# Linear attention over chunks: masked scores times v and q times the state, as one product over 128 rows

## The reference

```python
def _L0_attn_ref(x, W_attn, b_attn, W_proj, b_proj):      # 16 heads of 32, T = 1024 steps
    q, k, v = jnp.split(x @ W_attn + b_attn, 3, axis=-1)
    q = elu(to_heads(q)) + 1; k = elu(to_heads(k)) + 1; v = to_heads(v)
    def step(carry, inp):
        kv, ksum = carry
        qt, kt, vt = inp
        kv = kv + kt[..., :, None] * vt[..., None, :]
        ksum = ksum + kt
        num = jnp.einsum('bhi,bhij->bhj', qt, kv)
        den = jnp.einsum('bhi,bhi->bh', qt, ksum)[..., None] + EPS
        return ((kv, ksum), num / den)
    ...
    return y @ W_proj + b_proj
x = L0_attn_x                                             # (8, 1024, 512) f32
x = x + _L0_attn_ref(_layernorm(x), W_attn, b_attn, W_proj, b_proj)
x = x + _L0_ffn_ref(_layernorm(x), ffn_weight, ffn_bias)  # fp8-rounded x times fp8-rounded weight
```

## Time and profile before

| what | value |
|---|---|
| median of 3 runs | 1015.83 us (1012.76 to 1016.66) |
| the profiled execution | 1014.31 us, span 1012.6 us |
| PE busy | 982.0 us, 97% of the span |
| DVE, POOL, ACT busy | 701.7, 535.3, 463.6 us |
| mean granted clock of PE | 0.991 |

### The profile page before, as it was taken

The page is one execution under the profiler, slowest core; times in us unless marked ns, Lnnn a source line. Parts: engine busy times, 40 slices in busy tenths (PEclk is TensorE's granted clock), DMA queues, the critical chain, the costliest instruction groups (busy, mean ns, idle before and its releaser), DMA issues.

```text
span 1012.6 us, 43583 instructions
## 1 busy us (share of the span) xinstructions
PE 982.0 (97%) x19504; PEld 549.5 (54%) x19504; DVE 701.7 (69%) x1448; ACT 463.6 (46%) x714; POOL 535.3 (53%) x523
## 2 busy tenths in 40 slices
PE   5999999999999999999999999999999999999895
PEld 2454555555555555555555555555555555555552
DVE  6888677677767677676767767767776767754573
ACT  5753452544545364453535445254454535445222
POOL 3545675564565565465456456456456556533323
PEclk9999999999999999999999999999999999999997
DMA  8714334333334334334342244343332543322211
GB/s 271 113 35 80 94 76 81 86 77 84 80 75 91 75 75 94 72 83 88 71 96 74 71 93 79 78 88 75 83 83 75 90 77 75 81 44 54 55 35 48
DMA packets 185355, 82.51 MB, mean 81 GB/s; under 512 B 165840, under 2 KB 165840, under 8 KB 185168
## 3 DMA queue, kind: packets, MB, share of 16 engines
q1 hardware_dynamic: 185168, 79.73, 34.9%
HBM read 22.81 MB, written 16.78 MB: 39 GB/s over the span
## 4 chain that ended last, share of the span: by engine, by line
PE 91%; DVE 3%; POOL 2%; ACT 1%; issue 1%; DMA 0%; ACTq 0%; POOLq 0%
PE R L231 74%; PE S L231 15%; PE R L235 3%; POOL st L875 1%; DVE st L606 1%; DVE xs L696 0%; POOL xn L877 0%; POOL x L877 0%; DVE raw L800 0%; DMA xs<-in_L_attn_x 0%; POOL xs L918 0%; POOL sm L902 0%; DVE qk L629 0%; DVE wpl L778 0%; ACT qk L448 0%
## 5 line engine op out<-in xcount | busy, mean ns | idle before, releaser
L231 PE MATMUL R<-xt,wh 128*128 128x512 f16 x1024 | 306.2, 381 | 2.4 <-ACT wh L439 2.4
L629 DVE SCALAR_TENSOR_TENSOR qk<-qk,rel 128x512 f32<-128x512 f32 x128 | 141.3, 1105 | 151.1 <-ACT rel L451 151.1
L909 POOL TENSOR_TENSOR yhl<-y,yhl 128x512 f16<-128x512 f32 x60 | 69.9, 1165 | 311.2 <-ACT yhl L439 311.2
L231 PE MATMUL R<-xt,wl 128*128 128x512 f16 x512 | 194.4, 381 | 0.0
L875 POOL TENSOR_TENSOR st<-st,half 128x1 f32<-128x1 f32 x128 | 94.8, 741 | 138.3 <-DVE st L611 125.4
L231 PE MATMUL R<-wh,xt 128*128 128x512 f16 x512 | 160.3, 379 | 0.0
L231 PEld LDWEIGHTS R<-xt,wh 128*128 128x128 f16 x1024 | 96.7, 98 | 108.4 <-DVE xt L744 2.6
L231 PE MATMUL R<-wph,yt 128*128 128x512 f16 x512 | 134.6, 386 | 2.8 <-DVE yt L689 2.8
L439 ACT ACTIVATE yhl<-y 128x512 f16<-128x512 f32 x60 | 37.8, 630 | 209.5 <-DVE y L683 209.5
L448 ACT ACTIVATE qk<-R,bqk,wm 128x512 f32<-128x512 f32 x128 | 98.9, 772 | 54.0 <-PE R L231 54.0
L897 POOL TENSOR_TENSOR xs<-xs,bp 128x512 f32<-128x512 f32 x64 | 110.4, 1731 | 0.1
(11 more groups left out here) (91 smaller groups left out, 1498.0 us busy)
## 6 DMA issues: line engine op xcount, KB each, us to landing
xs<-in_L_attn_x SPq DMA_DIRECT2D x64, 256.0 KB, 3.8
out<-xs SPq DMA_DIRECT2D x64, 256.0 KB, 2.4
raw<-in_L_attn_W_attn SPq DMA_DIRECT2D x3, 1024.0 KB, 9.6
xs<-in_L_attn_W_proj SPq DMA_DIRECT2D x4, 256.0 KB
raw<-in_L_ffn_weight SPq DMA_DIRECT2D x1, 1024.0 KB, 16.2
x2t<-x2b SPq DMA_TRANSPOSE x62, 2.3
xt<-xnhl SPq DMA_TRANSPOSE x60, 3.1
yt<-yhl SPq DMA_TRANSPOSE x60, 3.2
```

What stands on the lines that cost most here:

```text
L231: return e.matmul(out, a, b, start=start, stop=stop, skip_group_check=True)
L629: e.scalar_tensor_tensor(qk[j % 2][:, i, :], qk[j % 2][:, i, :], 1.0, rel[:, (u - 1) % 2, :], ALU.min, ALU.add).then_inc(s_phi, 1)
L909: e.tensor_tensor(yhl[:, n % 2, 1, :], y[:, :], yhl[:, n % 2, 0, :], ALU.subtract).then_inc(s_yl, 1)
```

## The change

`from_state` goes. For each tile `sm` holds, for both halves a, 128 rows: in the 64 rows of the half itself the masked scores, and in the other 64 rows q (two heads' 32 rows one above the other). Facing them, v1 holds v in the 64 rows of the half and in the other 64 rows the state's 32 rows of the head, with zeros in the 32 rows of its neighbour. One product of 128 rows then gives both parts, and Y is written whole, 32 queries at a time: 64 products of 128 rows, 32 x 33.

- PE: `values(n)` is 64 such products (128 instructions); `from_state` (64 instructions, 32 in the first tile of a sequence) and the old `values` (64) are gone.
- DVE: `scores(n)` is two products of 64 partitions x 1024 columns, ahead of `ln1(n+8)`; `v_out` is two instructions of 64 partitions in place of one; y is one product of 128x512; `ln1_parts` moves to POOL. Between sequences the state is set to zero by a memset.
- ACT: the sm copy goes. `queries(n+1)` (four copies, 64 partitions x 512) stands behind the last phi of tile n and waits for `values(n)` on PE (`s_av`); `spread(n+1)` (eight copies, 32 partitions x 132) stands behind the copy of y and waits for mid and state of `update(n+1)` on DVE.
- POOL: the mask goes, `ln1_parts(n+8)` comes, behind `add_bp(n+8)`.
- `v1` is a ring of five tiles (NV) with a copy for each half; at the start POOL zeroes it whole and sets the ones. `sm` is now in the space of the raw v weights.

```diff
-            def from_state(n):
+            def values(n):
                 src, v, j, c = parts(n)
...
+                pe.wait_ge(s_smd, n + 1)
+                pe.wait_ge(s_q, n + 1)
+                pe.wait_ge(s_v, n + 1)
+                pe.wait_ge(s_spread, n + 1)
                 for g in range(4):
...
+                    for h in range(4):
+                        for i in range(4):
+                            a, b = divmod(i, 2)
+                            at = g * HALF + 32 * b
+                            mm = matmul(Y[32 * i:32 * i + 32, h, g * W:(g + 1) * W], sm[:, h, a, at:at + 32],
+                                        v[:, a, 4 * g + h, :], True, True)
                 mm.then_inc(s_av, 1)
...
@@ PE, in each tile
                 if n < NT:
                     scores(n)
-                    from_state(n)
                     ahead(chunks(n)[0])
...
@@ ACT
-            def scores(n):
-                if not alone(n):
-                    act.wait_ge(s_score, 4 * n + 4)
-                    if n:
-                        act.wait_ge(s_av, n)
-                    copy(sm[:, 2:4, :, :], scored(2)).then_inc(s_scopy, 1)
+            def queries(n):
+                src, v, j, c = parts(n)
+                for g in range(4):
+                    act.wait_ge(s_phi, phi_count(j, g))
+                act.wait_ge(s_wl, 6)
+                if n:
+                    act.wait_ge(s_av, n)
+                for a in range(2):
+                    for p in range(2):
+                        q = src[half_rows(p), 0:4, tokens(n, a)[0]].unsqueeze(1).broadcast_to([HALF, 2, 4, HALF])
+                        dst = sm[half_rows(1 - a), 2 * p:2 * p + 2, a, :].rearrange("p h (g t) -> p h g t", g=4)
+                        made = copy(dst, q)
+                made.then_inc(s_q, 1)
+            def spread(n):
+                v = v1[:, n % NV, :, :, :].rearrange("p a (g h) w -> p a g h w", g=4)
+                act.wait_ge(s_one, 2)
+                if n >= NV:
+                    act.wait_ge(s_av, n - NV + 1)
+                for a in range(2):
+                    act.wait_ge(*((s_mid, n + 1) if a else (s_state, n + 1)))
+                    held = mid if a else state[:, n % 2, :]
+                    for h in range(4):
+                        at, rows = HALF * (1 - a) + 32 * (h % 2), slice(32 * h, 32 * h + 32)
+                        made = copy(v[at:at + 32, a, :, h, :], held[rows, :].rearrange("p (g w) -> p g w", g=4))
+                made.then_inc(s_spread, 1)
...
@@ ACT, in each tile
-                    scores(n)
...
                     if n:
                         ahead(chunks(n)[1])
+                    if n + 1 < NT:
+                        queries(n + 1)
                     values(n)
                     if n == 0:
                         ahead(chunks(n)[1])
+                    if n + 1 < NT:
+                        spread(n + 1)
...
@@ DVE
             def scores(n):
...
+                for a in range(2):
+                    dst = sm[half_rows(a), :, a, :].rearrange("p h (g t) -> p h g t", g=4)
+                    made = e.tensor_tensor(dst, scored(a), causal_over(a), ALU.mult)
+                made.then_inc(s_smd, 1)
...
-                e.tensor_tensor(dst[:, 0:4:2, :, :], out[:, 0:4:2, :, 0:32],
-                                inv[:, 0:4:2, :, :].broadcast_to([P, 2, 4, 32]), ALU.mult)
...
+                e.tensor_tensor(dst, out[:, :, :, 0:32], inv.broadcast_to([P, 4, 4, 32]), ALU.mult).then_inc(s_y, 1)
...
@@ DVE, in each tile
                 if n < NT:
+                    scores(n)
                     if n + 8 < NT:
                         ln1(n + 8)
-                    scores(n)
...
-                    if n + 8 < NT:
-                        ln1_parts(n + 8)
...
@@ POOL
                     if n + 8 < NT:
                         ln1(n + 8)
-                    scores(n)
                     if n + 8 < NT:
                         add_bp(n + 8)
+                        ln1_parts(n + 8)
...
+            e.memset(v1[:, :, :, :, :], 0.0).then_inc(s_blank, 1)
```

More of the change, by code:

```diff
@@ L323, in scores @@
                             rows = slice(32 * h, 32 * h + 32)
-                            matmul(S[out, h, g * HALF:(g + 1) * HALF], src[rows, 4 + g, cols], src[rows, g, cols], True, True)
-            def from_state(n):
[L328 to L342, removed]
+                            mm = matmul(S[out, h, g * HALF:(g + 1) * HALF], src[rows, 4 + g, cols], src[rows, g, cols],
+                                        True, True)
@@ L344, in values @@
+                mm.then_inc(s_score, 1)
             def values(n):
                 src, v, j, c = parts(n)
-                first = n % PER == 0
-                pe.wait_ge(s_smd, masked_dve(n))
-                if not alone(n):
-                    pe.wait_ge(s_sel, n)
+                pe.wait_ge(s_smd, n + 1)
+                pe.wait_ge(s_q, n + 1)
                 pe.wait_ge(s_v, n + 1)
[L351 to L357, removed]
+                pe.wait_ge(s_spread, n + 1)
@@ L569, in _ @@
             phi(0, 7)
+            queries(0)
+            k_tokens(0)
             proj_size()
-            k_tokens(0)
             ffn_half()
@@ new lines, in v_out @@
+                dve.wait_ge(s_one, 2)
+                if n >= NV:
+                    dve.wait_ge(s_av, n - NV + 1)
+                for a in range(2):
+                    rows = half_rows(a)
+                    made = e.scalar_tensor_tensor(v1[rows, n % NV, a, :, 0:32], heads(bank["qkv", j, 8 + t][rows, :]),
+                                                  UN_V[rows], heads(bv[rows, :]), ALU.mult, ALU.add)
+                made.then_inc(s_v, 1)
+            def scores(n):
+                dve.wait_ge(s_score, n + 1)
+                dve.wait_ge(s_causal, 3)
+                if n:
+                    dve.wait_ge(s_av, n)
+                for a in range(2):
+                    dst = sm[half_rows(a), :, a, :].rearrange("p h (g t) -> p h g t", g=4)
+                    made = e.tensor_tensor(dst, scored(a), causal_over(a), ALU.mult)
+                made.then_inc(s_smd, 1)
@@ L658, in update @@
                 if n % PER < PER - 1:
                     dve.wait_ge(s_mid, n + 1)
-                    e.tensor_tensor(new, bank["delta", n, 1][:, 0:4 * W], mid[:, :], ALU.add).then_inc(s_state, 1)
+                    e.tensor_tensor(state[:, (n + 1) % 2, :], bank["delta", n, 1][:, 0:4 * W], mid[:, :],
+                                    ALU.add).then_inc(s_state, 1)
+                elif n + 1 < NT:
+                    e.memset(state[:, (n + 1) % 2, :], 0.0).then_inc(s_state, 1)
             def values(n):
@@ L897, in add_bp @@
                 e.tensor_tensor(x, x, bp[:, :], ALU.add).then_inc(s_xb, 1)
-            def scores(n):
-                if not alone(n):
-                    pool.wait_ge(s_scopy, n)
-                    e.tensor_tensor(sm[:, 2:4, :, :], sm[:, 2:4, :, :], causal_over(2), ALU.mult).then_inc(s_sel, 1)
             def values(n):
@@ L924, in _ @@
             e.memset(half[:, :], -0.5).then_inc(s_half, 1)
-            for i in range(2):
-                e.memset(v1[i][:, :, :, 32:33], 1.0).then_inc(s_one, 1)
             for m in range(4):
@@ L937, in _ @@
             pool.wait_ge(s_causal, 3)
+            e.memset(v1[:, :, :, :, :], 0.0).then_inc(s_blank, 1)
+            pool.wait_ge(s_blank, 1)
+            for a, base, step in ((0, -HALF, 1), (1, HALF - 1, -1)):
+                ones = v1[:, :, a, :, 32:33].rearrange("p i h w -> p (i w) h")
+                e.affine_select(out=ones, in_=ones, compare_op=ALU.is_ge, fill=1.0, base=base,
+                                pattern=[[0, NV], [0, 16]], channel_multiplier=step).then_inc(s_one, 1)
             ln1(4)
```

80 lines of the change are left out of this document (28 added, 52 removed).

## The result

The changed kernel takes **1087.27 us** (1085.91 to 1088.74) against 1014.3 us for the kernel before on the same chip: ratio 1.072 [1.069, 1.075], 73 us slower. The forecast was 998.5 us, in a range of 988 to 1037. The profiled execution takes 1086.11 us, its span is 1084.4 us and PE's mean granted clock 0.968 (0.991 before).

A forecast was written before the change was run, and what follows sets the result against it. PE, busy 97% of the span, was taken to bound the kernel: 21.3 us less on PE, 4 us more at start and tail, so 1015.8 - 17.3 = 998.5 us, range 988 to 1037.

The forecast's parts named there:

- the ACT and DVE loop: Waits from `values(n)` through ACT's copies, DVE, POOL and phi to the next `queries`: 14.6 to 16.0 us, priced at nothing.
- PE, what goes and comes: On PE, `from_state` saves 0.63 us a tile; new `values` takes 1.30 us (bounds 1.25 and 2.14), 0.23 more than before.
- B: Rival: PE's new `values` products run at about 16.7 ns each, 2.0 to 2.14 us; 1037 to 1047 us; 12%.
- D: Rival: on PE each weight load waits for the product before it, +2.6 us a tile; about 1165 us; 5%.
- the dear end: Upper estimate of the ACT and DVE loop, 16.0 us for a tile of 14.7 us.
- the middle, 15.3: Middle estimate of the ACT and DVE loop: slips 0.6 us in each of two tiles, won back in the other two.
- Rival C: The ACT loop binds at 16.0 us and PE waits for `ktok`, losing 3.5 to 15 us; 1002 to 1014 us; 17%.
- DVE, POOL: hidden,: DVE's work grows 0.3 us on 10.6 of 14.7 us a tile, POOL's does not matter; both hidden behind PE.
- Start and tail: First tiles and tiles 59 to 63: longer masks and waits cost +2.5 us and +3 with the tail's saving; together +4.
- E: Rival: better than forecast, `values` at 1.25 us and no loss at the ends; under 989 us; 6%.

The follow-up runs named there:

- the kernel without the copies: Changed kernel with ACT's q copies made only for tile 0 and state copies only for the first five v1 slots: 1057.3 us, ratio 1.042.
- the reordered kernel: Changed kernel with statistics ahead of masks on DVE and PE's order `values`, `proj`, `ffn`, `update`, scores; DVE and ACT in the same order: 986.95 us, ratio 0.972.
- the supply mended: Changed kernel with only `proj(n-1)` moved between `values(n)` and `update(n+1)` on PE: 1076.6 us, ratio 1.060; second run 1075.8 us.
- the loop opened as well: Changed kernel with DVE's statistics ahead of the masks and `proj` between `values` and `update` on PE: 1003.7 us, ratio 0.989.
- loop mended: Changed kernel with only the statistics of `ln1(n+8)` put ahead of the masks on DVE: 1075.3 us, ratio 1.059.
- halves: Changed kernel with statistics ahead of masks and `values` cut in two around the third projection piece: 1053.3 us, ratio 1.039; also without the copies, 1012.2 us.
- the old kernel made dense: Kernel before the change with only `proj(n-1)` moved ahead of `update(n+1)`, so short products stand together: 1037.7 us, ratio 1.023.

## Why the prediction was wrong

Direction and size were wrong: faster by 17 us forecast, slower by 73 measured. Two steps failed, each enough to turn the sign: the ACT and DVE loop was taken at nothing, and the supply of PE's program was not in the sum at all. Point by point:

- **PE, what goes and comes: right.** Scores alone 0.84 us as priced; `values` 1.23 us for 1.30, just under its best bound, with a mean weight load of 109 ns where the old 64 columns took 134. Undisturbed tiles take 14.63 us in the kernel without the copies, and the mean tile is 14.61 us in the reordered kernel, 0.43 less than before, for a forecast of 0.38. So B and D are refuted: 128 products that all take the full 128 rows take 1.23 us, 10 ns each, less than a tenth of one load, so loads do not wait for the product before them. By the bullet of the Trainium skill that D leaned on (TensorE: Matmul & The Clock Gate, Part 3, The mechanism) a load overlaps a matmul only where the row group differs. The measurement decides against it for this shape; the same section's text also lets a load run ahead that goes to the background weight buffer, and that would fit.
- **The failed step, first half: "So I take nothing for it in the steady stretch", on a loop of "14.6 to 16.0 us".** The loop is 17.04 us. Of the 1.1 us over the dear end 0.9 lie in two terms that stood in the sum as single values: the residual sum, 1.2 us in this turn (mean 0.89) for 0.65, and POOL's power, 0.94 and 0.09 of hand-over, for 0.65. The copies, which had bounds, came out a little above their upper ones: 2.57 us for four of q with no overlap, 2.61 for eight of state. The forecast itself rested on the middle, 15.3, with the k copy ready at 10.4 us and wanted at 10.5: a margin of 0.1 us against bounds 1.4 us apart. And the slip is not won back as I assumed: in a tile in which the loop has slack, PE itself takes 14.6 us and the loop can't run ahead of it. With the supply mended the mean tile is 16.06 us against 14.87 with the loop opened as well, 65 us in 55 tiles, and the time 1077 us against 1004. Some of that may be the low clock that comes with the waits: PE is busy 982.8 us there against 967.1.
- **The failed step, second half: not in the prediction.** Of PE's 192 short products in a row I priced each and did not ask whether they can be supplied. The sign was there: "before" has one idle spot of 1.9 us with "issue" ahead of it in the middle of the `ktok` group of tile 59. By itself (loop mended) it makes 1004 into 1075 us: in the profiled executions 45 us idle and 23 us more of busy time, about what the low clock is worth.
- **The two cover each other.** Either alone costs 71 to 73 us, both together 84. A PE stall is hidden where PE would have waited for the loop, and the other way about. So each mended alone gives back only 11 or 12 us, and would have passed for a small matter.
- **Rival C** named the right place and wait (`R<-v,ktok` waits for ACT, 27 times, 34.4 us) and the wrong size, 1002 to 1014 us: its dear end was 16.0 us for the loop, and it spread the excess over four tiles.
- **DVE, POOL: hidden,** as far as sums go; masks 1218 ns for 1.19 us. **Start and tail:** +11.2 us for +4, the start +6.6 and the tail +4.6. With the statistics first alone they are -0.9 and +4.5, with `proj` between alone +5.4 and 0: the start goes with the masks' place on DVE, the tail with PE's order.
- **The chances.** "Faster 0.71, same 0.10, slower 0.19" does not follow from the ones listed: the forecast, E and half of C make 0.745, the other half 0.085, B and D 0.17. It changes nothing in the verdict.

That the change itself is sound, and lost to where its pieces stood, is shown by the kernels with the same work at 1004 and 987 us. That the stalls are the program's arrival is shown by position (192 in a row: stalls; 12 long products between, or halves: none of over 0.5 us; the old kernel made dense: stalls), by the timing of q8's packets and by the place of every stall in the count by 256. Open are why a packet starts sometimes before and sometimes up to some 2 us after the instructions ahead of it begin, whether the other queues have a part in that, and why the residual sum is slow in the changed kernel.

## What to carry to other kernels

When a change adds work to an engine "in the shadow", write the loop of waits from one tile to the next, put bounds on every term of it and not only on the new ones, and compare its dear end with the tile: a loop that is longer in some tiles is paid in those, not averaged away. When a change makes PE's instructions shorter, count how many stand in a row and how long a packet's worth of them (128 products here) lasts, beside the 2 to 3 us that the next packet takes; long products between them cost nothing here. Where two waits may cover each other, mend both before judging either.

## What the runs showed of the hardware

- Products of 128 rows x 32 columns in f32 with 33 moving columns run at 10 ns each over four column places (128 in 1.23 us), as fast as those of 64 rows (64 in 0.69 us with the changeover).
- Each gap of PE with "issue" as its releaser was, in these kernels between 107 and 890 us, late program, of up to 2.7 us, at a step of 256 records, one packet of 16.4 KB on q8.
- The low clock followed 12 of the 21 gaps with the statistics first, for 3.4 or 6.8 us, and 2 of 15 in the dense old kernel, its longest of 1.4 us; two gaps of 2.2 us without the copies (ending at 212.53 and 775.64) were not followed by it.
- Copies on ACT of 64 partitions x 512 stand at their full 628 ns one behind the other (409.05 to 411.59 for four), where one of 128 x 512 took 597 to 630; those of 32 partitions x 132 took 313 ns, what 132 columns were priced at. Fewer partitions saved nothing.
- DVE's residual sum took 676 ns in the reordered kernel and 893 in the changed one; the one at 398.51 took 1.25 us while POOL's sum of the same shape ran (397.94 to 399.21). That the two disturb each other is likely and was not isolated.
